# Attention scores from float32r stacks of 48 and 50 rows, two heads on the halves of the array's rows, and the causal mask inside VectorE's row maximum

## The reference, cut to what matters

```python
# x: (4, 1024, 256) float32
xn = _layernorm(x)
q, k, v = split(xn @ w_qkv)            # 16 heads of 16 numbers each
scores = einsum('bqhd,bkhd->bhqk', q / 4, k)
scores = where(key <= query, scores, -1e10)   # causal mask
s = (softmax(scores) @ v) @ w_out
h = xn
for i in range(6):                     # 256 -> 1024 -> 256
    h = gelu(h @ W1[i].T + B1[i]) @ W2[i].T + B2[i] + h
    if i < 5: h = layernorm(h) * LN_G[i] + LN_B[i]
return x + s * silu(h)
```

## Time and profile before

| | us |
|---|---|
| median of 3 runs | 1800.6 (1800.38 to 1801.91) |
| span of the profiled execution, first to last instruction | 1806.1 |
| TensorE busy | 1716.2 (95%) |
| VectorE busy | 1149.1 (64%) |
| ScalarE busy | 958.0 (53%) |
| GpSimd busy | 323.2 (18%) |

### The profile page before, as it was taken

How to read it: one execution, slowest core, us unless ns; L and a number is a source line. 1 busy time by engine, 2 the same in 40 slices (tenths; PEclk the granted TensorE clock), 3 DMA queues, 4 the chain that set the end, 5 groups by cost and what they waited for, 6 DMA issues and landing times. The chain is left out here.

```text
span 1806.1 us, 33624 instructions
## 1 busy us (share of the span) xinstructions
PE 1716.2 (95%) x11664; PEld 1312.9 (73%) x11664; DVE 1149.1 (64%) x2325; ACT 958.0 (53%) x1364; POOL 323.2 (18%) x317
## 2 busy tenths in 40 slices
PE   6979999999999999999999999997999989999947
PEld 5869999999999989999999998875444433444236
DVE  7846666666666656666666643366877866877326
ACT  5834555555555545555555554432666665666723
POOL 3511111111111111111111111110121211121214
PEclk9989999999999999999999999998999998999969
DMA  6940000000000000000000050003474754574113
GB/s 206 306 140 13 12 17 16 13 12 17 13 9 12 17 16 12 13 17 12 16 12 12 0 83 24 23 24 64 76 112 75 109 84 73 88 107 73 48 57 137
DMA packets 104427, 97.97 MB, mean 54 GB/s; under 512 B 26636, under 2 KB 88588, under 8 KB 104316
## 3 DMA queue, kind: packets, MB, share of 16 engines
q1 hardware_dynamic: 104256, 96.39, 23.9%
q10 hardware_dynamic: 60, 0.10, 0.0%
HBM read 62.15 MB, written 29.62 MB: 51 GB/s over the span
## 5 line engine op out<-in xcount | busy, mean ns | idle before, releaser
L626 ACT ACTIVATE m_hid<-m_h_ps,m_b1s 128x512 f32<-128x512 f32 x384 | 264.3, 688 | 571.0 <-PE m_h_ps L752 558.9
L687 DVE TENSOR_TENSOR m_hidl<-m_hid,m_hidh 128x512 fp32r<-128x512 f32 x384 | 307.4, 809 | 323.9 <-ACT m_hidh L628 322.8
L129 DVE TENSOR_REDUCE mx<-a_s_ps 128x1 f32<-128x512 f32 (+3 forms) x570 | 341.2, 656 | 91.3 <-PE a_s_ps L117 87.8
L1003 ACT ACTIVATE a_prob<-a_st_ps 128x1024 f32<-128x1024 f32 (+1 forms) x320 | 289.9, 938 | 168.5 <-PE a_st_ps L1153 123.0
L752 PE MATMUL m_h_ps<-xth,shared 128*128 (+1 forms) x768 | 269.8, 397 | 12.3 <-DVE shared L655 12.2
L763 PE MATMUL m_y_ps<-shared,m_hidh 128*128 128x256 f32 x1536 | 277.9, 281 | 0.0
L628 ACT ACTIVATE m_hidh<-m_h_ps,m_b1s 128x512 fp32r<-128x512 f32 x384 | 261.8, 682 | 0.0
L763 PEld LDWEIGHTS m_y_ps<-shared,m_hidh 128*128 128x128 f32 x1536 | 246.6, 189 | 12.0 <-DVE m_hidl L687 0.4
L602 POOL TENSOR_TENSOR y<-y,m_b2s 128x1024 f32<-128x1024 f32 x47 | 112.8, 2400 | 708.3 <-DVE y L663 708.3
L763 PE MATMUL m_y_ps<-m_w2h,m_hidh 128*128 128x256 f32 x768 | 217.9, 284 | 0.6 <-DVE m_hidl L687 0.3
L763 PE MATMUL m_y_ps<-shared,m_hidl 128*128 128x256 f32 x768 | 215.8, 281 | 0.0
(11 more groups left out here) (115 smaller groups left out, 2648.3 us busy)
## 6 DMA issues: line engine op xcount, KB each, us to landing
q_parts<-p_part SPq DMA_DIRECT2D x16, 384.0 KB, 3.5
k_parts<-p_part SPq DMA_DIRECT2D x16, 384.0 KB, 3.0
m_raw<-w1t SPq DMA_DIRECT2D x48, 128.0 KB, 2.2
m_raw<-w2t SPq DMA_DIRECT2D x48, 128.0 KB, 2.4
shared<-q_parts SPq DMA_DIRECT2D x48, 128.0 KB, 4.6
shared<-k_parts SPq DMA_DIRECT2D x48, 128.0 KB, 7.7
a_qs<-q_parts SPq DMA_DIRECT2D x48, 128.0 KB, 4.6
a_ks<-k_parts SPq DMA_DIRECT2D x48, 128.0 KB, 7.4
```

The costliest lines, as they stand in the source:

```text
L129: return nc.vector.reduce_max(mx[:, half, first:first + heads, qt], scores, AX_X)
L626: nc.scalar.activation(hid[k % 2][:], h_ps[k % 2][:], ACT.Gelu, bias=b1s[s.par][:, k:k + 1])
L687: nc.vector.tensor_tensor(hidl[k % 4][:], hid[k % 2][:], hidh[k % 4][:].bitcast(F32), ALU.subtract).then_inc(low_done, 1)
L1003: nc.scalar.activation(prob[step % BUFS][:, j:j + heads, 0:hi - lo], unit_ps(unit), ACT.Exp).then_inc(exp_done, 1)
```

## The change

- q and k are stored in two float32r parts instead of three bfloat16 parts: ScalarE writes the first, VectorE the second. ScalarE's and GpSimd's further splits and the tile `rest` go.
- A stack has 3 x 16 = 48 rows (50 in the second pass). Heads 0 and 1 of a group lie on the partitions from 0, heads 2 and 3 on those from 64. Matmuls come in pairs, one for each half (a *side*), each into a bank of its own. `LOADS` stays 12.
- A piece now takes two banks, one per side: 20 pieces make a group. The three banks are still used in turn, so a piece shares one bank with the piece before it. `piece` waits until the first side of the piece before is reduced.
- The mask matmul goes. On a diagonal piece VectorE runs `tensor_tensor_reduce` (add the tile `causal`, then maximum) once for each head; elsewhere `reduce_max` once for each side. `tensor_tensor_reduce` also writes a bfloat16 tile `unused`.
- `EARLY` becomes 6, `TURN` 4, `CHAIN` 3; the maxima go out in four DMAs instead of three. `pace` follows one `bank_free`.
- `groups` writes all 16 groups out; the loop goes.
- In `mlp`, a piece of group 0 waits until both sides of the piece before are reduced.

```diff
@@ -40,11 +40,13 @@
 HG = 4
 QT = SEQ // P
 BANK = 512
-PARTS = 3
-STACK = 6 * HD
+PARTS = 2
+STACK = 3 * HD
 ROWS = STACK + PARTS
-EARLY = 10
-TURN = 6
+SIDE = P // 2
+PAIR = 2
+EARLY = 6
+TURN = 4
 DVE_COLUMN, DVE_START = 2.5, 150
 ACT_COLUMN, ACT_START = 2.0, 500
...
-            heads = min(BANK // keys, HG)
-            pieces += [(qt, half, j, heads, keys) for j in range(0, HG, heads)]
+            columns = min(BANK // keys, PAIR)
+            pieces += [(qt, half, c, columns, keys) for c in range(0, PAIR, columns)]
     return pieces
 def load_stacks(sp, scratch, to_q, to_k, bt, hg, loaded):
-    for to, src, order in ((to_q, scratch["q"], (0, 0, 0, 1, 1, 2)), (to_k, scratch["k"], (0, 1, 2, 0, 1, 0))):
-        for r, part in enumerate(order):
-            rows = src[HG * HD * hg:HG * HD * (hg + 1), part, bass.ds(SEQ * bt, SEQ)].rearrange("(h d) n -> d h n", d=HD)
-            sp.dma_start(to[r * HD:(r + 1) * HD, :, :], rows).then_inc(loaded, 16)
+    for to, src, order in ((to_q, scratch["q"], (0, 0, 1)), (to_k, scratch["k"], (0, 1, 0))):
+        for side in range(2):
+            first = HG * HD * hg + PAIR * HD * side
+            for r, part in enumerate(order):
+                rows = src[first:first + PAIR * HD, part, bass.ds(SEQ * bt, SEQ)].rearrange("(c d) n -> d c n", d=HD)
...
 def piece_products(nc, to, q, k, piece, keep):
-    qt, half, first, heads, keys = piece
-    diagonal = qt // HG == half
-    for j in range(heads):
-        i = nc.tensor.matmul(to[:, j, :], q[0:STACK, first + j, qt * P:(qt + 1) * P],
-                             k[0:STACK, first + j, half * BANK:half * BANK + keys], start=True, stop=not diagonal)
-        if diagonal:
-            i = nc.tensor.matmul(to[:, j, keys - P:keys], keep["identb"][:], keep["maskb"][:], start=False, stop=True)
+    qt, half, first, columns, keys = piece
+    for c in range(columns):
+        for side in range(2):
+            rows = slice(SIDE * side, SIDE * side + STACK)
+            i = nc.tensor.matmul(to[side][:, c, :], q[rows, first + c, qt * P:(qt + 1) * P],
+                                 k[rows, first + c, half * BANK:half * BANK + keys], start=True, stop=True)
     return i
-def by_head(bank, piece):
-
-    _, _, _, heads, keys = piece
-    return bank[:, 0:heads * keys].rearrange("p (h n) -> p h n", n=keys)
-
-
-def row_max(nc, mx, scores, piece):
-    qt, half, first, heads, _ = piece
-    return nc.vector.reduce_max(mx[:, half, first:first + heads, qt], scores, AX_X)
+def by_column(bank, piece):
+
+    _, _, _, columns, keys = piece
+    return bank[:, 0:columns * keys].rearrange("p (c n) -> p c n", n=keys)
+
+
+def row_max(nc, mx, scores, piece, side, unused):
+
+    qt, half, first, columns, keys = piece
+    unused, causal = unused
+    to = mx[:, half, PAIR * side + first:PAIR * side + first + columns, qt]
+    if qt // HG != half:
+        return nc.vector.reduce_max(to, scores, AX_X)
+    for c in range(columns):
+        i = nc.vector.tensor_tensor_reduce(unused[:, side, c * keys:(c + 1) * keys], scores[:, c, :], causal[:, BANK - keys:BANK], 1.0, NEG,
+                                           ALU.add, ALU.max, to[:, c:c + 1])
+    return i
...
@@ -299,11 +298,10 @@
                 dve.wait_ge(gtl_stored[u], 16 * n)
                 nc.vector.tensor_tensor(gtl[u][:], tr_ps[:], gth[u][:].bitcast(F32), ALU.subtract).then_inc(low_done, 1)
-            def split_rest(g, m):
+            def split_low(g, m):
                 dve.wait_ge(part0_done, 4 * g + m + 1)
-                dve.wait_ge(part2_done, 4 * g + m + 1)
-                nc.vector.scalar_tensor_tensor(rest[m][:], qk_ps[m][:], 0.25 if m < 2 else 1.0,
-                                               part[m][:, 0, :], ALU.mult, ALU.subtract).then_inc(rest_done, 1)
+                nc.vector.scalar_tensor_tensor(part[m][:, 1, :], qk_ps[m][:], 0.25 if m < 2 else 1.0,
+                                               part[m][:, 0, :].bitcast(F32), ALU.mult, ALU.subtract).then_inc(part1_done, 1)
             statistics(0, 0, 1)
             norm(0, 0, 1)
...
@@ -769,9 +760,9 @@
                     if p == 0:
                         pe.wait_ge(stacks_loaded, 2 * LOADS * 16)
                         pe.wait_ge(xtl_done, GROUPS * (BLOCKS - 1) + 1)
-                    if p >= 2:
-                        pe.wait_ge(piece_maxed, p - 1)
-                    to = by_head(tr_ps[:, p % 2, :], PIECES[p])
+                    if p >= 1:
+                        pe.wait_ge(piece_maxed, 2 * p)
+                    to = [by_column(tr_ps[:, side, :], PIECES[p]) for side in range(2)]
                     piece_products(nc, to, *stacks[0], PIECES[p], keep).then_inc(piece_done, 1)
                 if s.kind != "first":
...
@@ -869,30 +860,34 @@
         def unit_ps(unit):
-            step, _, heads = UNITS[unit]
+            step, _, columns = UNITS[unit]
             _, _, lo, hi = STEPS[step]
-            pitch = BANK if heads == 2 else hi - lo
-            return st_ps[unit % 2][:, 0:heads * pitch].rearrange("p (h n) -> p h n", n=pitch)[:, :, 0:hi - lo]
-
-
-        assert (NP + 1) % BANKS == 0
+            return st_ps[unit % 2][:, :, 0:columns * (hi - lo)].rearrange("p s (c n) -> p s c n", n=hi - lo)
+
+        def unit_prob(unit):
+
+            step, first, columns = UNITS[unit]
+            _, _, lo, hi = STEPS[step]
+            by_side = prob[step % BUFS][:].rearrange("p (s c) n -> p s c n", s=2)
+            return by_side[:, :, first:first + columns, 0:hi - lo]
+
+        PLACES = 2 * (NP + 1)
+        assert PLACES % BANKS == 0
         def piece_ps(p):
-            return by_head(s_ps[(p + (p >= TURN)) % BANKS], PIECES[p])
-
-        turned = s_ps[TURN % BANKS][:].bitcast(BF16)[0:PARTS * HG * QT, 0:P]
+            place = 2 * (p + (p >= TURN))
+            return [by_column(s_ps[(place + side) % BANKS], PIECES[p]) for side in range(2)]
+
+        turned = s_ps[2 * TURN % BANKS][0:PARTS * HG * QT, 0:P]
         def groups(eng, body):
-            for hg in range(HG):
-                body(0, hg, hg > 0, 2)
-            with eng.Fori(1, BATCH - 1) as bt:
+            for bt in range(BATCH):
                 for hg in range(HG):
-                    body(bt, hg, True, 2)
-            for hg in range(HG):
-                body(BATCH - 1, hg, True, min(2, HG - 1 - hg))
+                    n = HG * bt + hg
+                    body(bt, hg, n > 0, min(2, N_GROUPS - 1 - n))
         @block.sync
...
@@ -904,9 +899,11 @@
             def store_max(n, slot):
                 sp.wait_ge(nmt_ready, n + 2)
                 for part in range(PARTS):
-                    src = nmt[part * HG * QT:(part + 1) * HG * QT, :]
-                    dst = qs[slot][STACK + part:STACK + part + 1, :, :].rearrange("a h (t q) -> a (h t) q", q=P)
-                    sp.dma_start(dst, src).then_inc(nm_stored, 16)
+                    for side in range(2):
+                        first = part * HG * QT + side * PAIR * QT
+                        row = SIDE * side + STACK + part
+                        dst = qs[slot][row:row + 1, :, :].rearrange("a c (t q) -> a (c t) q", q=P)
+                        sp.dma_start(dst.bitcast(F32), nmt[first:first + PAIR * QT, :]).then_inc(nm_stored, 16)
             def store_o(n, bt, hg):
                 wait_apart(sp, o_copied, 2 * n + 3, sp_passed)
...
+            dve.sem_inc(nm_stored, NM_DMAS * 16)
+            dve.sem_inc(piece_maxed, 2 * NP + 1)
             def piece_max(n, hg, p):
                 dve.wait_ge(piece_done, NP * n + p + 1)
-                row_max(nc, mx[hg % 2], piece_ps(p), PIECES[p]).then_inc(piece_maxed, 1)
+                for side in range(2):
+                    row_max(nc, mx[hg % 2], piece_ps(p)[side], PIECES[p], side, (unused[:, p % 2], keep["causal"])).then_inc(piece_maxed, 1)
             def negate_step(n, hg, step):
...
@@ -1084,17 +1079,17 @@
             pe.sem_inc(piece_done, NP)
             def piece(n, hg, p):
-                if p == TURN + BANKS - 1:
+                if p == TURN:
                     pe.wait_ge(nmt_ready, n + 1)
-                pe.wait_ge(piece_maxed, NP * n + p + (2 if TURN <= p < TURN + BANKS - 1 else 1))
+                pe.wait_ge(piece_maxed, 2 * (NP * n + p) + (1 if p == TURN else 0))
                 piece_products(nc, piece_ps(p), qs[hg % HG], ks[hg % HG], PIECES[p], keep).then_inc(piece_done, 1)
             def transpose_max(n, hg, more):
                 pe.wait_ge(nm_ready, n + 1)
                 if more:
-                    pe.wait_ge(piece_maxed, NP * (n + 1) + TURN + 1)
-                nc.tensor.transpose(turned, nm[:].rearrange("p a m -> p (a m)"), identb[:]).then_inc(nmt_done, 1)
+                    pe.wait_ge(piece_maxed, 2 * (NP * (n + 1) + TURN - 1) + 1)
+                nc.tensor.transpose(turned, nm[:].rearrange("p a m -> p (a m)"), ident[:]).then_inc(nmt_done, 1)
             def search(bt, hg, p, follow):
...
                 turn = 0
-                now = dve_free = act_free = 0
```

(62 more changed lines are left out.)

84 lines of the change are left out of this document (37 added, 47 removed).

## The result

The kernel after takes 1951.6 us at the median of four executions (1936.5 to 1958.3), the kernel before 1801.3 beside it: a ratio of 1.082, 95% interval 1.077 to 1.086. Forecast were 1895 and a range of 1835 to 1960. Kernels whose TensorE clock falls in some groups and not in others differ by up to 2.4% between their own executions, so small effects are read from periods inside one trace.

What follows compares the result with a forecast made beforehand. TensorE's columns were taken to bound `attend` (28.1 of 28.67 us a group). Profiled 1806.1 plus 86 (periods), -1 (last groups), +5 (`project`), +4 (`mlp`) gave 1900; less 5.5 for profile over median, 1895 us, range 1835 to 1960.

Steps and rivals of the forecast that it cites:

- three parts in series: Period in `attend`: second pass 21.6, tail up to transpose 6.3, transpose to landing 5.1 us; 33.0, stated as 33.3.
- the clock: TensorE in `attend`: half clock in every group's idle tail, ten cold microseconds, +2.7 a period to 36.0; ends 0 and +10.
- `project` and `mlp`: Stages outside `attend`: `project` +5 us from larger q and k parts, search in `mlp` +4 us, ends 0 and 10.
- Pairs: TensorE search and second-pass scores: two row halves work at once, 0.23 us a pair; 0.46 if in series.
- The rival of halves in series: TensorE row halves do not overlap, pairs cost 0.46 us, total 1902, up to 1960 with the clock; 10% chance.
- The new reduction: VectorE diagonal pieces in `attend`: each `tensor_tensor_reduce` costs +0.06 us over a plain reduction, 32 a group.
- Two cycles a number: Rival on VectorE's new reduction: tail pieces cost 6.4 us more, period 39.7 warm, total 1947; 9% chance.
- Seven pieces left, a tail in series: `pace` in `attend`: 13 of 20 turns fit the second pass, seven follow alone; 6.3 us to the transpose, then 5.1.
- the 1.0 for the way back between pieces: Tail in `attend`: about 0.25 us lost between half a piece reduced and the next ready, four times.
- The 24% for a clock that stays up: Rival in `attend`: the tail costs but the clock stays; period 33.3 us, total 1857; 24% chance.
- Last two groups: End of `attend`: the last two groups change by -1 us, being bound by ScalarE.
- The loop: Loop over sequences in `attend`: writing it out removes 5.24 us idle and 16 us at half clock, about 13 us.

Runs made afterwards that it cites:

- the clock held: Kernel after plus unread matmuls in idle TensorE time: three pairs ahead of each late piece but the first, seven behind the last; 1873.2 us, ratio 1.038.
- mask alone: Kernel before, loop written out, mask matmuls replaced by masked reduction per head, bfloat16 stacks and one-bank pieces kept; 1773.8 us, ratio 0.984.
- turns released evenly: Two kernels: after with search turns released every 2,200 columns, 1851.5 us; also with eight early pieces, two maxima DMAs, waiting only for first-stack ones, 1922.6 us.

## Why the prediction was right, and where it was off

The mechanism held (seven pieces left behind the pass, three parts in series, the clock falling in every group), the forecast came out 57 us below the measured time, and the term that was mis-sized is the clock: how long it stays low. Nearly all of it lies in the 14 periods of 39.2 instead of 36.0 (+45) and in the end (+14); `project` and `mlp` came out 3 lower than said.

- *Pairs.* Said 0.23, in series 0.46. The seven added pairs took 1.78 us together; in the trace the two matmuls of a pair start 3 to 4 ns apart. The rival of halves in series is out.
- *The new reduction.* Said +0.06 for each. Timelines show 0.61 us from start to start at 512 numbers beside 0.60 of the plain one, and the runs 0.14 a group for the twelve in series: five to six times too dear, 0.6 us of the tail. Two cycles a number is out.
- *Seven pieces left, a tail in series.* As said, down to which pieces: five until the transpose, two behind it. In after the transpose comes 6.6 us behind the last scores (said 6.3 behind the pass) and the next scores 5.1 behind the transpose (said 5.1). With the clock held the pass itself is 21.2 (said 21.6), tail and wait are 7.1 and 4.4. Period at full clock: said 33.3, measured 32.7 steady, 33.0 as a mean. That the tail came out so close is partly luck: the 1.0 for the way back between pieces and the 0.6 for dear reductions were not there (the four pieces and the chain took 5.0 on VectorE, with stops of 0.1), and the 1.3 us that VectorE still needs for the last piece of the pass were not in the sum. The prediction also counted 10 pairs, 2.3 us, of TensorE's work in tail and wait; the trace has 9, most of them shorter than 512 columns, 3,072 columns or 1.4 us.
- *The clock.* Said: falls in every tail, ten microseconds, +2.7. It does fall in every period, but only two of the fifteen get by with 10 us low; ten have over 20, the mean behind the first is 22.7, and the mean price is +6.0. The wrong step is the ten microseconds, "well into the second pass": where only 10 were low the period was 34.4, +1.7 over 32.7, less than said. The ends that I gave for the price, 0 and +10, held it; the value taken did not. A pass with the low clock lasts up to 30.5 us instead of 21.2. What decides how long it stays low no run shows. With +6.0 in place of +2.7 the forecast would have been 14 x 3.3 = 46 higher, 1941, against 1951.6. The 24% for a clock that stays up are answered by the run with the clock held: 1873, where the text said 1857.
- *Last two groups.* Said -1, came +12.9 with the end of the kernel: I took ScalarE for their bound; they have tail and low clock as all others (38.2 us for the last period, 31.0 with the clock held, 27.1 before).
- *The start of `attend`.* The first period is 42.4 instead of 32.0. It has the low clock too, but also a part not costed: eight DMAs of ones on ScalarE's queue instead of four, with the first scores behind them (`[1.74 <-DMA a_ks<-a_ones]`): 10.4 us from the end of the first copy to the first scores, 6.9 in before.
- *`project` and `mlp`.* Said +5 and +4, came +6.4 together. The DMA queue in `project` carries 19.05 MB in 12,183 packets in the window of the earlier trace rows, at 98.8%: per busy time 7% more bytes than before's 16.83 MB in 15,489 packets. How the 6.4 divide between the two stages was not measured.
- *The loop.* Said 13; the kernel before with the loop written out took 1793.7 beside 1804.5: 10.8. Its copies stand 28.6 to 28.7 apart, behind the first period and up to the last.

## What to carry to other kernels

When a change takes work off the engine that hides another's, redo the schedule for the new lengths: an order that releases work by a planner's idea of the other engine leaves it to the end as soon as the pass that should hide it (here the second pass on TensorE) gets shorter than the work to be hidden (here VectorE's reductions). Test that suspicion by putting the order into the old kernel, and separate it from the clock by filling idle TensorE time with matmuls that nobody reads. And do the parts one at a time: here the mask in the reduction and the written-out loop are worth 1.6%, and what is left, the row halves with their pieces of two banks, their `EARLY` and DMAs, takes away more than that. That VectorE was too close behind TensorE (24.1 of 27.35 us busy with the mask alone) for TensorE's columns to be worth much is my reading; no run has the row halves by themselves.

## What was not expected of the hardware

- Half clock is not a matter of long stillness only. With turns released evenly TensorE is busy for 23.2 to 23.6 of 28.7 us and never idle for more than 0.8 at a time (read from single records of whole periods), and yet the clock fell in nine and in twelve of fifteen periods, at 1434.9 us in the one kernel and at 1387.8 in the other, out of such periods. At 29.7 of 32.7 (clock held) and 26.8 of 27.35 (mask alone) it stayed up in the steady part. The busy share alone does not tell: with two DMAs and the same added matmuls TensorE is busy for 29.4 of 32.15 us, stops for 0.65 at most as with four DMAs, and yet the clock fell for 3.4 us in five of the thirteen periods behind the first. What decides stays open. The Trainium skill (TensorE: Matmul & The Clock Gate, A second HAM failure mode: psum-queue depth-cycling) tells of a kernel whose clock swings because TensorE stops briefly and often between groups of matmuls; the two traces with turns released evenly agree that short stops, here 0.8 us at most, can go with a clock that swings.
- The step that delivers the accumulator of `tensor_tensor_reduce` has its own record of 0.08 us (at 1358.57 above), and the distance of two such instructions is only 0.01 over that of plain ones: it lies beside the next one. The Trainium skill (VectorE: DVE Perf Modes, Two Vector instructions with no wait between them) counts two instructions; the trace has both, and the second is free here.
- The two row halves load their weights at the same time as well: in the added matmuls at 1462.22 the records of a pair's two loads start 3 ns apart, and pairs with both loads follow each other every 0.23 us.
